# A two-layer attention and mixture-of-experts kernel on one core: row maxima by halves of the maps, the first norm by pairs of tiles, layer 1 begun beside the last shared experts

## What is computed

```python
x = L0_attn_x
xn = _layernorm(x)
s = attention0(xn)        # 16 heads, 2 maps each (32 maps), softmax(QK1) - lam*softmax(QK2), head norm, @ Wo
g = _silu(ffn0(xn))       # 16 experts top-2 (inner 176) + 2 shared experts
x = x + s * g
xn = _layernorm(x)
s = attention1(xn)        # 16 heads (16 maps), rotary, causal softmax, @ Wo + bo
g = _silu(ffn1(xn))       # 8 experts, top-1, capacity 160, gelu
x = x + s * g
```

## Time and profile before

| what | value |
|---|---|
| median of 3 runs | 574.97 us (574.58 to 576.38) |
| the profiled execution's own time | 576.48 us |
| its span in the profile | 574.7 us |
| TensorE busy | 481.3 us, 84% |
| VectorE busy | 336.2 us, 59% |
| ScalarE busy | 245.3 us, 43% |
| GpSimd busy | 173.3 us, 30% |
| chain that ended last | PE 55%, DVE 17%, POOL 13%, issue 9%, ACT 3%, DMA 1% |

### The profile page before, as it was taken

How to read it: one execution, slowest core, us unless ns; L and a number is a source line. 1 busy time by engine, 2 the same in 40 slices (tenths; PEclk the granted TensorE clock), 3 DMA queues, 4 the chain that set the end, 5 groups by cost and what they waited for, 6 DMA issues and landing times.

```text
span 574.7 us, 11343 instructions
## 1 busy us (share of the span) xinstructions
PE 481.3 (84%) x4128; PEld 327.6 (57%) x4128; DVE 336.2 (59%) x867; ACT 245.3 (43%) x459; POOL 173.3 (30%) x225
## 2 busy tenths in 40 slices
PE   1577899997799898899999998649778899989961
PEld 0354766563466554577777776328545566767540
DVE  4589778777656833064422348753796768621335
ACT  1052363672367566633433323112424555654222
POOL 3343303208474406041000074080232635110114
PEclk9889789999799999999999999775778999999985
DMA  8894000002011032423323251610000103000104
GB/s 301 274 420 111 3 4 2 4 2 76 20 58 40 2 79 51 126 59 111 104 81 110 64 193 56 233 60 1 0 3 11 35 15 113 3 3 20 48 27 147
DMA packets 28511, 44.11 MB, mean 77 GB/s; under 512 B 5666, under 2 KB 24866, under 8 KB 27170
## 3 DMA queue, kind: packets, MB, share of 16 engines
q1 hardware_dynamic: 26153, 37.09, 20.1%
q0 software_dynamic: 2304, 6.29, 3.5%
HBM read 28.13 MB, written 14.94 MB: 75 GB/s over the span
## 4 chain that ended last, share of the span: by engine, by line
PE 55%; DVE 17%; POOL 13%; issue 9%; ACT 3%; DMA 1%; POOLq 0%; DVEq 0%; ACTq 0%
PE bank L896 9%; PE bank L918 6%; PE bank L707 5%; PE bank L792 4%; PE bank L697 4%; PE bank L799 4%; DVE work L1368 4%; PE bank L751 3%; PE bank L731 3%; PE bank L819 3%; PE bank L841 3%; POOL x_slots L1178 3%; PE bank L727 2%; PE bank L754 2%; PE bank L684 2%
## 5 line engine op out<-in xcount | busy, mean ns | idle before, releaser
L980 ACT ACTIVATE work<-bank 96x1024 bf16<-96x1024 bf16 (+4 forms) x180 | 102.8, 582 | 128.5 <-PE bank L707 79.9
L1368 DVE TENSOR_REDUCE work<-bank 128x2 f32<-128x512 f32 (+1 forms) x144 | 97.2, 686 | 41.0 <-PE bank L731 39.3
L1023 ACT ACTIVATE work<-bank 128x512 f32<-128x512 f32 x144 | 83.1, 595 | 70.8 <-PE bank L754 35.6
L707 PE MATMUL bank<-identb,work 128*96 128x128 bf16 x576 | 51.6, 244 | 20.8 <-POOL work L1144 10.8
L727 PE MATMUL bank<-neg_ts,identb 128*128 128x256 bf16 (+1 forms) x144 | 47.9, 333 | 19.3 <-DVE work L1368 17.8
L707 PEld LDWEIGHTS bank<-identb,work 128*96 128x96 bf16 x576 | 45.5, 143 | 25.3 <-POOL work L1144 12.6
L697 PE MATMUL bank<-wqkv,xnT 128*128 128x512 f32 (+1 forms) x128 | 53.6, 554 | 1.9 <-ACT xnT L980 1.4
L1135 POOL COPY work<-work 128x1024 bf16<-128x1024 bf16 (+1 forms) x16 | 16.4, 1024 | 124.2 <-DVE work L1355 124.1
L1671 DVE TENSOR_TENSOR work<-work,bank 128x176 f32<-128x176 f32 x47 | 15.9, 337 | 59.8 <-ACT work L1075 59.4
L799 PE MATMUL bank<-work,cst 128*32 128x256 f32 (+1 forms) x768 | 49.5, 330 | 0.0
L751 PE MATMUL bank<-identb,neg_ts 128*128 128x256 bf16 x144 | 45.3, 315 | 4.8 <-ACT work L1023 4.1
(11 more groups left out here) (205 smaller groups left out, 840.0 us busy)
## 6 DMA issues: line engine op xcount, KB each, us to landing
moe<-w_in SPq DMA_DIRECT2D x6, 1056.0 KB, 11.1
x_slots<-wo SPq DMA_DIRECT2D x41, 128.0 KB, 1.9
work<-x_slots SPq DMA_DIRECT2D x31, 128.0 KB, 2.2
y_slots<-work SPq DMA_DIRECT2D x31, 128.0 KB, 1.7
moe<-f1a_in SPq DMA_DIRECT2D x1, 2048.0 KB, 8.3
moe<-f1b_in SPq DMA_DIRECT2D x1, 2048.0 KB, 12.8
moe<-w_in SPq DMA_DIRECT2D x2, 880.0 KB
wqkv<-wqkv_in SPq DMA_DIRECT2D x2, 768.0 KB, 5.4
```

The lines of the kernel that those rows point to most:

```text
L707: mm = nc.tensor.transpose(bfv(a.pj.bank(key))[0:STACK, u, :], stack[:, 8 * g + u].rearrange("p s d -> p (s d)"), identb[:, :])
L980: return nc.scalar.activation(dst, src, ACT.Copy)
L1023: nc.scalar.activation(pT[at % 6], a.st.bank(w)[:, :], ACT.Exp, scale=SCALE)\
L1368: nc.vector.tensor_reduce(nmax[:, ms[0]:ms[-1] + 1], a.s.bank((b, q))[:, :].rearrange("p (m s) -> p m s", s=n), AX_X, ALU.max, negate=True ...
```

## The change

1. **Row maxima by halves of the maps.** The maxima of one sequence are taken in two *shares*. A share is one half of the maps (16 of 32, or 8 of 16) for both of its tiles. The rows of a share go out when it is done, and an exp waits only for its own share's rows. The table moves the exps forward against the maxima.
2. **Homes.** Layer 0 has two homes instead of three, so all of `w2` can be loaded at the start; the late loads are gone. Layer 1 keeps three, in another order; `y_back`, `xs1T` and `y_back1` change places.
3. **First norm by pairs.** x comes in four transfers of two tiles, the identity and `wqkv` directly behind the first; norms go by pairs, in both layers (power on two columns, eight powers and eight `newton` in all where there were four).
4. **Layer 1's exps without their mask.** The 48 mask matmuls L751 of layer 1 go. GpSimd cuts the exponentials instead: 48 AFFINE_SELECTs on `pT`, which write zero where the key is later than the query; `value` waits for the unit's third one.
5. **Layer 1 begun early.** The steps of layer 1's beats 0 to 9 run in turns 44 to 51 of `experts0`, on all engines. The ones and zeros of the first home are set beforehand, those of the others behind the second norm.
6. TensorE waits for the last use of two banks when layer 0's remaining steps are done (turn `len(tail)`), SP loads layer 1's expert weights after the last combination.

The core of the diff:

```diff
-    dict(x=(0, 18, 29, 30), settle=(11, 11, 17, 20, 25, 30),
...
-         maxima=14, rows=(9, 25), exps=43, values=4,
+    dict(x=(0, 16, 29, 29), settle=(5, 5, 7, 11, 15, 18, 20, 26),
...
+         maxima=17, rows=(12, 25), exps=34, values=4,
-         maxima=9, rows=(6, 12), exps=24, values=4,
+         maxima=10, rows=(6, 12), exps=20, values=5,
...
+         early=(44, 0, 3, 4, 4, 5, 9, 9, 10)),
...
+            a.by_share = [q for g in range(a.shares) for half in range(HALVES)
+                          for q in ((range(u), range(u, 3 * u))[half])[g * u * (half + 1) // a.shares:
+                                                                      (g + 1) * u * (half + 1) // a.shares]]
...
-                for beat in range(beats):
-                    put(here + c["maxima"] + beat, "max", (b, beat))
+                for beat, q in enumerate(a.by_share):
+                    put(here + c["maxima"] + beat, "max", (b, q))
...
+            for k, beat in enumerate(c.get("early", ())[1:]):
+                upto = sum(map(len, line[:beat]))
+                a.early[c["early"][0] + k], done = steps[done:upto], upto
...
+            x_pair(0)
+            sp.dma_start(cst[:, 0:C_ROPE], consts_d[:, 0:C_ROPE]).then_inc(ld["ident"], 16)
+            for k in range(KD):
+                sp.dma_start(wqkv[:, k], wqkv0_d[:, k]).then_inc(ld["wqkv"], 16)
...
                 if u == 0:
-                    pe.wait_ge(a.rows[b % 2], 16 * PARTS * HALVES * (b // 2 + 1))
+                    pe.wait_ge(a.rows[b % 2][4 * j // a.share], 16 * PARTS * (b // 2 + 1))
...
-                nc.tensor.matmul(view[:, :, 0:P], neg_ts[:, :], identb[:, :].unsqueeze(1).to_broadcast([P, len(ms), P]),
-                                 start=True, stop=False, skip_group_check=True)
                 if a.n == 0:
+                    nc.tensor.matmul(view[:, :, 0:P], neg_ts[:, :],
+                                     identb[:, :].unsqueeze(1).to_broadcast([P, len(ms), P]),
+                                     start=True, stop=False, skip_group_check=True)
...
-                pe.wait_ge(*a.st.emptied((b, j, 2)))
+                pe.wait_ge(*(a.st.emptied((b, j, 2)) if a.n == 0 else (a.cut, a.st.at[(b, j, 2)] + 1)))
...
-                for n in range(N0 + 2):
+                for n in range(N0 + 6):
                     attention(attns[0], beside_experts(attns[0], n))
+                    if n == len(attns[0].tail):
+                        attns[0].pj.wait_drained(pe)
+                    if n == min(attns[1].early):
+                        pe.wait_ge(ld["wqkv1"], 16)
+                    attention(attns[1], early_beside(n))
...
+                    elif kind == "exp" and a.n == 1:
+
+                        maps, n = (2, SEQ) if w[2] < 2 else (4, P)
+                        pool.wait_ge(*a.st.emptied(w))
+                        probs = pT[a.st.at[w] % 6].rearrange("p (m t) -> p m t", t=n)[:, :, 0:P]
+                        nc.gpsimd.affine_select(probs, probs, [[0, maps], [1, P]], ALU.is_ge, zero_fill, base=0,
+                                                channel_multiplier=-1).then_inc(a.cut, 1)
+                        if w[2] == 2:
+                            pool.wait_ge(a.cut, a.st.at[w] + 1)
...
-            layer_norm(norms[1])
+            for n in range(N0 + 6):
+                attention(attns[1], early_beside(n))
+                for i in back_at(n, 2):
+                    if i % 2:
+                        layer_norm(norms[1], (i // 2,))
+                    if i == 1:
+                        ones_beside(attns[1], (0,), 2)
```

269 lines of the change are left out of this document (148 added, 121 removed).

## The result

| | before | changed |
|---|---|---|
| median, same chip | 575.67 us (574.58 to 576.75, 4 runs) | 569.77 us (569.31 to 571.23, 4 runs) |
| ratio, 95% interval | | 0.9902 [0.9872, 0.9931] |
| profiled execution, its span | 576.48, 574.7 us | 569.31, 567.5 us |

The change is faster by 5.9 us in the medians and by 7.2 between the two profiled executions. The forecast was 553, with 540 to 566: the sign was right, the size was not, and the time lies outside the range.

A forecast was written before the change was run, and what follows sets the result against it. TensorE, busy 84%, was taken to bound the kernel, with idle time outside the routed experts. Terms -2.0 - 3.7 - 3.4 + 0.5 - 9.6 - 6.9 + 3.0 = -22.1 gave 553 us against the median, range 540 to 566.

The forecast's parts named there:

- What bounds the kernel: Whole kernel: TensorE busy 84% of the span, without slack in the routed experts; elsewhere idle time and low clock can be gained.
- The start, -2.0: Start of layer 0: smaller first transfer and statistics of two tiles fewer bring the first projection sooner, bounds 0 and -3.5.
- Shares, layer 0, -3.7: Before layer 0's first exp: twelve of 29 maxima move behind it, so exps fill idle TensorE time; bounds 0 and -8.9.
- the fourth rival, homes: Layer 0: with two homes the exps do not shift forward, -3.7 becomes +4, time 561; chance 0.10.
- Experts of layer 0, +0.5: Layer 0's experts: the new wait for two banks' last use adds ScalarE's last copy, bounds 0 and +1.
- Layer 1 begun early, -9.6: From 338 us to layer 1's first maximum: 13.0 us sooner, less 3.4 for the router; bounds -4 and -18.
- The halving of the router's matmuls: Layer 1: the router's 32 matmuls, 6.83 us at low clock, cost half at full clock behind the first maximum: +3.4.
- The second rival: Shared experts: early steps lengthen them by as much as moves there, -13 becomes -5, time 561; chance 0.20.
- Shares, layer 1, -3.4: Layer 1, 403.3 to 440 us: five of 15 maxima move behind the first exp, saving a third of 10.1 us idle.
- Masks -6.9, cuts +3.0: Layer 1's 16 units: masks removed save 0.43 us each, mostly where TensorE is bound; late GpSimd cuts cost 3.0, bounds 0 and +8.
- Rival 1: Layer 1 before the experts: cuts queued on GpSimd hold TensorE 3 us in each of 12 units, time 586; chance 0.05.
- the +8 for the cuts: Layer 1: upper bound on the cuts' cost, also holding 3.0 us of VectorE casts slowed beside GpSimd.

The follow-up runs named there:

- e7: e1 with layer 0's first norm over four tiles in place of pairs: 562.18 us, ratio 0.9783.
- e1: The changed kernel with only its three w2 loads moved behind the first four shares' rows: 563.69 us, ratio 0.9795.
- e13: e1 run again on another chip: 560.29 us, ratio 0.9768.
- e3: The changed kernel with no step of layer 1 begun early beside the shared experts; norm by pairs and early memsets stay: 581.99 us, ratio 1.0133.
- e5: e1 with layer 1's maxima taken again by tiles over all maps, its exponentials later: 567.93 us, ratio 0.9885.
- e2: The changed kernel with layer 1's masks back on TensorE and no cuts on GpSimd: 573.48 us, ratio 0.9979.
- e16: e1 without cuts on GpSimd and without masks in layer 1, so its causal restriction is left out: 561.3 us, ratio 0.9789.
- e14: e1 with layer 1's row maxima in one bf16 part, the other two parts zeros set once: 557.29 us, ratio 0.9692.
- e4: The changed kernel with layer 1's rows turned two beats later: 578.37 us, ratio 1.0049.
- e8: e1 with layer 1's rows and exponentials both one beat later: 565.96 us, ratio 0.9858.

## Why the prediction was wrong, step by step

- **What bounds the kernel**: right. TensorE is idle where the change acts, and not in the routed experts: busy for 81.9 of 82.6 us there.
- **The start, -2.0**: the statistics came as worked out and the landing sooner (3.60 for 4.68), the first projection even 3.3 us. The sentence that VectorE "does there what it did later" is the one that failed: the power of the second pair stands behind the spreading, and the gain is spent by the first maximum (e7: 0).
- **Shares, layer 0, -3.7**: with `w2` out of the way, layer 0 with the start gives -6.7 in e1's profile and -10.5 in e13's; with the projections put back this is -3.5 and -7.3, against -5.2 forecast, so the profiles do not show this term too large. The step that failed is the sentence on the late `w2` loads, "which costs nothing either way": I looked for who waits for `w2`, and not for what waits behind it in SP's queue. It cost 6 us (e1's 563.7 and the changed kernel's 569.8). Nothing in TensorE's waits points to the fourth rival, homes; no run changed their number.
- **Experts of layer 0, +0.5**: nothing of it shows. The routed experts took 3.2 us more, and 16 matmuls of the output projection, 1.73 us for each eight, are that much. The prediction took 338 us for their end; the last routed expert's up ends at 322.1, and what follows are shared experts.
- **Layer 1 begun early, -9.6**: -9.8 at the tenth maximum, where the router's logits lie behind in both kernels. That these agree is luck, since 3.2 us of layer 0's work have moved into the stretch. With these put back it is -13.0, some 1 us of it the router's last steps that moved out, and e3 says -12.8 for the early turns alone: the mechanism was right, the term some 2 to 3 us too small. The halving of the router's matmuls came as worked out (3.64 for 6.83). The second rival's mechanism is real: from the last routed to the last shared expert's up it is 38.4 us before, 46.9 in the changed kernel and 43.3 in e3, which has no early step at all but the pairs' norm products between the experts. It did not decide, since these 8.5 us are less than the beginning saves.
- **Shares, layer 1, -3.4**: e5 says -4.2. Right when undone alone, with layer 1 begun early, by two medians from different chips.
- **Masks -6.9, cuts +3.0**: together -3.9, measured -3.7 (e2). Singly both were off by about 3: the cuts cost nothing (e16), the masks were worth 3.7. The spacing of 0.11 and 0.21 us is a mask's price in TensorE's busy time, and e2 shows it there in full (5.3 us in the middle). The step that failed is "mostly so before": in the middle TensorE waits for 14.8 of 90 us, and 2.7 us of the price go into time in which it would have waited. Rival 1 is refuted: no wait of TensorE in the changed kernel names a cut. Its two thirds for GpSimd's load are 56% (60.8 of 107.7 us).
- **The middle of layer 1**: here lies the largest error, 11.5 us, and no term covered it. Beyond the shares, the masks and the cuts the forecast let nothing change in this stretch. The sentence that failed is "The new row instructions are as many as before": I counted the row instructions and not their place. They stand closer to the last maximum and next to GpSimd's spreading, and TensorE waits 10.8 us for the parts in place of 2.7. Against this stand 3.3 us of waits for the spreading that went, so idle time grew by 4.8. About 2 us are work that moved in, and the lower granted clock, 0.92 in place of 0.98, can be up to some 5 us. The contention of VectorE with GpSimd was weighed for casts beside the cuts, 3.0 us, and lay with the spreading. Shortening the row steps gave back 3 us (e14); giving them slack gave nothing (e4, e8). So the row steps are shown for 3 us, and the cause of the rest stays open. Why the shares and the masks gain when undone one by one, and the stretch is still slower than before, is not settled; no run put the old layer 1 order whole into the new kernel.
- **The range**: most costs had their bounds, but not the masks nor layer 1's shares, and the +8 for the cuts was the only one on the slow side that came behind the tenth maximum.

## What to carry to other kernels

Before a load is moved to the front of a queue, ask what small transfer will stand behind it; that nobody waits for the load itself says nothing. When steps are reordered, count not their number but the distance from each step to the step that it waits for, and what the other engine does at that moment. When two orders are compared by landmarks, check that the same work lies between them. Removing one wait at a time shows whether a stretch is bound by that wait or only passes it on; and the numbers that a softmax subtracts need no more precision than keeps its exponents small.
